# Cross attention in a decoder: scores seven pairs ahead, another order of transfers, and all key parts on POOL

## The reference

```python
Q = (query @ Wq + bq).reshape(B, Sq, H, D).transpose(0, 2, 1, 3)
K = (key @ Wk + bk).reshape(B, Sk, H, D).transpose(0, 2, 1, 3)
V = (value @ Wv + bv).reshape(B, Sk, H, D).transpose(0, 2, 1, 3)
scores = jnp.einsum('bhqd,bhkd->bhqk', Q, K) / jnp.sqrt(jnp.float32(D))
attn = jax.nn.softmax(scores, axis=-1)
out = jnp.einsum('bhqk,bhkd->bhqd', attn, V)
return out.transpose(0, 2, 1, 3).reshape(B, Sq, E) @ Wo + bo
```

## Time and profile before

| | us |
|---|---|
| median of three runs | 4712.51 (4709.47 to 4729.79) |
| the profiled execution | 4729.11 |
| its span | 4727.3 |
| PE busy | 3885.6 |
| DVE busy | 2978.1 |
| ACT busy | 2181.7 |
| POOL busy | 1144.9 |

### The profile page before, as it was taken

The page is one execution under the profiler, slowest core; times in us unless marked ns, Lnnn a source line. Parts: engine busy times, 40 slices in busy tenths (PEclk is TensorE's granted clock), DMA queues, the critical chain, the costliest instruction groups (busy, mean ns, idle before and its releaser), DMA issues. The chain is left out here.

```text
span 4727.3 us, 107462 instructions
## 1 busy us (share of the span) xinstructions
PE 3885.6 (82%) x44766; PEld 2680.4 (57%) x44766; DVE 2978.1 (63%) x4986; ACT 2181.7 (46%) x2885; POOL 1144.9 (24%) x1441
## 2 busy tenths in 40 slices
PE   7987559999996977799999979866779999995498
PEld 5864226666664446466666654333346666663376
DVE  5632468877774445488777743355668787773643
ACT  2234436656663233266666643433346666663010
POOL 0000024444440000144444410021434444430000
PEclk9989869999997999899999989978789999996689
DMA  3035035555551410355555511000045555550366
GB/s 131 0 117 201 2 88 134 139 133 137 136 135 33 115 45 0 68 140 134 139 138 138 135 44 63 24 4 4 0 108 141 134 140 137 137 129 1 81 178 159
DMA packets 251804, 463.48 MB, mean 98 GB/s; under 512 B 135598, under 2 KB 143278, under 8 KB 251086
## 3 DMA queue, kind: packets, MB, share of 16 engines
q1 hardware_dynamic: 251406, 457.76, 38.1%
HBM read 212.85 MB, written 1.72 MB: 45 GB/s over the span
## 5 line engine op out<-in xcount | busy, mean ns | idle before, releaser
L1326 DVE TENSOR_REDUCE x_bank_top<-ps 112x1 f32<-112x500 f32 x2304 | 1409.7, 670 | 457.9 <-PE ps L1055 446.2
L1184 ACT ACTIVATE x_probs_t<-ps 128x1344 f32<-128x1344 f32 x768 | 990.9, 1290 | 309.1 <-PE ps L1072 296.3
L1055 PE MATMUL ps<-x_keys,x_queries 96*112 96x500 bf16 x2304 | 697.2, 387 | 62.8 <-DVE x_bank_top L1326 34.7
L1072 PEld LDWEIGHTS ps<-x_queries,x_keys 128*128 128x128 bf16 x9216 | 504.1, 98 | 189.6 <-ACT x_probs_t L1184 90.6
L1072 PE MATMUL ps<-x_queries,x_keys 128*128 128x112 bf16 x9216 | 585.8, 213 | 30.9 <-ACT x_probs_t L1184 25.0
L1055 PEld LDWEIGHTS ps<-x_keys,x_queries 96*112 96x112 bf16 x2304 | 288.7, 131 | 391.9 <-DVE x_bank_top L1326 198.2
L1085 PE MATMUL ps<-x_probs_t,x_values 128*32 128x112 f32 x18432 | 491.2, 263 | 4.1 <-ACT x_probs_t L1184 4.1
L1085 PEld LDWEIGHTS ps<-x_probs_t,x_values 128*32 128x32 f32 x18432 | 444.4, 111 | 51.0 <-issue 43.0
L1250 POOL TENSOR_TENSOR x_key_part<-x_key_whole,x_nothing 128x500 bf16<-128x500 f32 x186 | 231.3, 1244 | 826.0 <-ACT x_key_whole L1171 826.0
L1034 PE MATMUL ps<-x_ctx_t,x_wk 128*128 128x500 f32 x558 | 311.3, 640 | 25.5 <-ACT x_key_whole L1171 15.5
L1045 PE MATMUL ps<-x_wv,x_ctx_t 128*128 128x128 f32 (+1 forms) x2304 | 328.8, 286 | 1.7 <-issue 1.6
(11 more groups left out here) (478 smaller groups left out, 5340.2 us busy)
## 6 DMA issues: line engine op xcount, KB each, us to landing
x_keys<-x_key_part SPq DMA_DIRECT2D x1152, 192.0 KB, 3.5
x_ctx_t<-in_ctx_t SPq DMA_DIRECT2D x96, 750.0 KB, 4.6
cm_ctx_n<-in_ctx_n SPq DMA_DIRECT2D x32, 768.0 KB, 6.0
cm_ctx_t<-in_ctx_t SPq DMA_DIRECT2D x32, 750.0 KB, 8.3
x_queries<-x_query_part SPq DMA_DIRECT2D x1152, 14.0 KB, 2.3
e_share<-m_weight_scratch SPq DMA_DIRECT2D x32, 490.0 KB
e_spread_out<-m_slot_scratch SPq DMA_DIRECT2D x32, 490.0 KB
e_share<-m_weight_rows SPq DMA_DIRECT2D x32, 448.0 KB, 5.8
```

Source lines behind the costliest of these rows:

```text
L1055: nc.tensor.matmul(ps[0:RW, n, 0:KB], queries[i % 2][0:TALL, p, :], keys[i % 2][0:TALL, p, KB * n:KB * n + KB], start=True, stop=True).the ...
L1072: mm = nc.tensor.matmul(ps[:, TURNED + c // VC, RW * (c % VC):RW * (c % VC) + RW], keys[i % 2][:, p, KT * c:KT * c + KT], queries[i % 2][: ...
L1184: nc.scalar.activation(probs_t[PROBS[p]].rearrange("k (n c) r -> k n (c r)", c=VC), ps[:, TURNED:TURNED + VR, 0:VC * RW], ACT.Exp, scale=s ...
L1326: nc.vector.tensor_reduce(bank_top[0:RW, p, n:n + 1], ps[0:RW, n, 0:KB], AX_X, ALU.max).then_inc(topped, 1)
```

## The change

- `LEAD` is 7 instead of 6; maxima are turned in steps 2 and 6.
- Keys are projected three batches ahead (i+3 in pass i), in steps 5 to 7 behind the scores; values of i+1 move to steps 1 to 3. Passes begin at -2.
- All three thirds are split by POOL, the maxima of half 1 between the second and the third. `last_parts` on DVE goes. POOL waits, before it writes the key parts of i, until the stack of i-2 has landed.
- Keys and queries have stacks and semaphores of their own. Queries are stacked for two batches in one transfer; in the first pass half of those transfers are issued by ACT.
- SP's order is new (below).

```diff
-LEAD = 6
+LEAD = 7
...
-    KEY_STEPS, VALUE_STEPS, FOLD_STEP = (1, 2, 3), (5, 6, 7), 4
-    BY_POOL = NB_ - 1
+    VALUE_STEPS, FOLD_STEP, KEY_STEPS = (1, 2, 3), 4, (5, 6, 7)
...
+        def query_slots(engine, e, h, s):
+
+            source = slice(64 * h, 64 * h + 64)
+            queries_of = query_parts[QUERY_PART[s]][source]
+            engine.dma_start(queries[e % 2][s:TALL:SLOTS, HP_ * h:HP_ * h + HP_].rearrange("r p b n -> r (p b n)"),
+                             queries_of[:, 2 * e:2 * e + 2].rearrange("f b c s -> f (b c s)")).then_inc(queries_stacked[e % 2][h], 16)
...
-            def stack(i, h):
+            def stack_keys(i, h):
 
                 u = i % 2
                 wait(sp, turned_done, PR * (i - 2) + HP_ * (h + 1))
                 if i == 0:
                     sp.wait_ge(lead_low, NB_)
                 else:
-                    sp.wait_ge(k_low, BY_POOL * i)
-                    sp.wait_ge(last_low, i)
+                    sp.wait_ge(k_low, NB_ * i)
...
+            def stack_queries(e, h):
+
+                wait(sp, turned_done, PR * (2 * e - 3) + HP_ * (h + 1))
+                sp.wait_ge(q_low, 2 * (2 * e // CB) + 2)
                 for s in range(SLOTS):
...
+                    query_slots(sp, e, h, s)
...
             def one_pass(i):
-                if has(i + 3):
-                    context(i + 3)
+                if i % 2 == 1 and has(i + 1):
+                    stack_queries((i + 1) // 2, 1)
                 if has(i + 2):
-                    for h in range(2):
-                        stack(i + 2, h)
-            for i in range(-1, B):
+                    stack_keys(i + 2, 0)
+                if has(i + CONTEXTS):
+                    context(i + CONTEXTS)
+                if i % 2 == 0 and has(i + 2):
+                    stack_queries(i // 2 + 1, 0)
+                if has(i + 2):
+                    stack_keys(i + 2, 1)
+            for i in range(B):
                 one_pass(i)
...
-                    wait(pe, added, min((i - 3) // CB, CH - 1))
+                    wait(pe, mix_kept, i - 3)
...
-                    if step == 3 and has(i):
+                    if step == 2 and has(i):
                         turn_tops(i, 1)
-                    if step == 7 and has(i + 1):
+                    if step == 6 and has(i + 1):
                         turn_tops(i + 1, 0)
-                    if step in KEY_STEPS and has(i + 2):
-                        make_keys(i + 2, KEY_STEPS.index(step))
+                    if step in VALUE_STEPS and has(i + 1):
+                        make_values(i + 1, VALUE_STEPS.index(step))
                     if step == FOLD_STEP and has(i - 1):
                         fold(i - 1)
-                    if step in VALUE_STEPS and has(i + 1):
-                        make_values(i + 1, VALUE_STEPS.index(step))
                     ahead, pair = divmod(step + LEAD, PR)
                     if has(i + ahead):
                         scores(i + ahead, pair)
+                    if step in KEY_STEPS and has(i + 3):
+                        make_keys(i + 3, KEY_STEPS.index(step))
...
+            act.wait_ge(q_low, 2)
+            for s in range(SLOTS):
+                query_slots(act, 0, 0, s)
...
+            def key_third(i, n):
+
+                part, cols, before = key_parts[i % 2], slice(KB * n, KB * n + KB), NB_ * (i - 1) + n
+                pool.wait_ge(k_kept, before + 1)
+                if n == 0:
+                    wait(pool, keys_stacked[i % 2][1], SLOTS * 16 * (i // 2))
...
             def one_pass(i):
...
                 if has(i + 1):
                     split_tops(i + 1, 0)
+                if has(i + 3):
+                    key_third(i + 3, 0)
+                    key_third(i + 3, 1)
+                if has(i + 1):
+                    split_tops(i + 1, 1)
+                if has(i + 3):
+                    key_third(i + 3, 2)
```

More of the change, by code:

```diff
@@ L908, in cross_attention @@
     ctx_landed = [chip.sem(tag + "ctx_landed%d" % u) for u in range(CONTEXTS)]
-    stacked = [[chip.sem(tag + "stacked%d_%d" % (u, h)) for h in range(2)] for u in range(2)]
+    keys_stacked, queries_stacked = ([[chip.sem(tag + "%s_stacked%d_%d" % (k, u, h)) for h in range(2)] for u in range(2)] for k in ("keys", "queries"))
     lead_done, lead_high, lead_rest, lead_mid, lead_low = (chip.sem(tag + k) for k in ("lead_done", "lead_high", "lead_rest", "lead_mid", "lead_low"))
@@ L944, in cross_attention @@
         key_whole = [sbuf("key_whole%d" % n, [P, KB]) for n in range(NB_)]
-        key_left = [sbuf("key_left%d" % n, [P, KB]) for n in range(2)]
+        key_left = sbuf("key_left", [P, KB])
         nothing = sbuf("nothing", [P, KB])
         keys = [sbuf("keys%d" % u, [P, PR, WIDE], BF16) for u in range(2)]
-        queries = [sbuf("queries%d" % u, [P, PR, RW], BF16) for u in range(2)]
+        queries = [sbuf("queries%d" % u, [P, PR, 2, RW], BF16) for u in range(2)]
         values = [sbuf("values%d" % u, [KT, NC_, VW]) for u in range(2)]
@@ L1005, in _ @@
                 load(dst[:], weight(name), rest_landed)
+            context(2)
             sp.wait_ge(zeros_ready, 2 * PARTS)
-            for h in range(2):
-                stack(0, h)
+            stack_keys(0, 0)
+            stack_keys(0, 1)
+            stack_queries(0, 1)
+            stack_keys(1, 0)
+            stack_keys(1, 1)
             def one_pass(i):
-                if has(i + 3):
-                    context(i + 3)
+                if i % 2 == 1 and has(i + 1):
+                    stack_queries((i + 1) // 2, 1)
                 if has(i + 2):
-                    for h in range(2):
-                        stack(i + 2, h)
-            for i in range(-1, B):
+                    stack_keys(i + 2, 0)
[6 more added lines that the diff above has]
+            for i in range(B):
                 one_pass(i)
@@ L1039, in make_values @@
                     pe.wait_ge(k_kept, NB_ * min(i + 1, B - 1))
-                    wait(pe, mix_kept, i - 1)
+                    wait(pe, mix_kept, i - 2)
+                    wait(pe, added, (i - 2) // CB)
                 else:
@@ L1049, in scores @@
                 if p % HP_ == 0:
-                    pe.wait_ge(stacked[i % 2][p // HP_], 2 * SLOTS * 16 * (i // 2 + 1))
+                    pe.wait_ge(keys_stacked[i % 2][p // HP_], SLOTS * 16 * (i // 2 + 1))
+                    if i % 2 == 0:
+                        pe.wait_ge(queries_stacked[i // 2 % 2][p // HP_], SLOTS * 16 * (i // 4 + 1))
                 if i == 0 and p == 0:
@@ L1072, in scores_by_key @@
                     mm = nc.tensor.matmul(ps[:, TURNED + c // VC, RW * (c % VC):RW * (c % VC) + RW],
-                                          keys[i % 2][:, p, KT * c:KT * c + KT], queries[i % 2][:, p, :], start=True, stop=True)
+                                          keys[i % 2][:, p, KT * c:KT * c + KT], queries[i // 2 % 2][:, p, i % 2, :], start=True, stop=True)
                 mm.then_inc(turned_done, 1)
@@ L1103, in project @@
                 pe.wait_ge(biased, c + 1)
[L1104 removed]
+                pe.wait_ge(k_kept, NB_ * min(CB * c + CB + 3, B - 1))
                 nc.tensor.matmul(ps[:, TURNS, 0:CT], wo[:], mix[:, CB * c:CB * c + CB, :].rearrange("p b s -> p (b s)"),
@@ L1144, in one_pass @@
                         mix_values(i, 0)
-            for i in range(-1, B + 1):
+            for i in range(-2, B + 1):
                 one_pass(i)
@@ L1166, in keep_keys @@
                 act.wait_ge(k_done, NB_ * (i - 1) + n + 1)
[L1167 to L1170, removed]
+                if i == 1:
+                    act.wait_ge(lead_low, n + 1)
+                wait(act, k_low, NB_ * (i - 2) + n + 1)
                 nc.scalar.activation(key_whole[n][:], ps[:, TURNS, 0:KB], ACT.Identity, bias=bk[:, 0:1]).then_inc(k_kept, 1)
@@ L1220, in one_pass @@
                         mid_query(i // 2 + 1)
-                    if step in KEY_STEPS and has(i + 2):
-                        keep_keys(i + 2, KEY_STEPS.index(step))
+                    if step in KEY_STEPS and has(i + 3):
+                        keep_keys(i + 3, KEY_STEPS.index(step))
                     if step in VALUE_STEPS and has(i + 1):
                         keep_values(i + 1, VALUE_STEPS.index(step))
-            for i in range(-1, B + 1):
+            for i in range(-2, B + 1):
                 one_pass(i)
@@ L1256, in low_parts @@
                 pool.wait_ge(k_rest, before + 1)
-                nc.gpsimd.tensor_tensor(part[1][:, cols], key_left[0][:], nothing[:], ALU.add).then_inc(k_mid, 1)
+                nc.gpsimd.tensor_tensor(part[1][:, cols], key_left[:], nothing[:], ALU.add).then_inc(k_mid, 1)
                 pool.wait_ge(k_mid, before + 1)
-                nc.gpsimd.tensor_tensor(part[2][:, cols], key_left[0][:], part[1][:, cols], ALU.subtract).then_inc(k_low, 1)
+                nc.gpsimd.tensor_tensor(part[2][:, cols], key_left[:], part[1][:, cols], ALU.subtract).then_inc(k_low, 1)
@@ L1280, in _ @@
```

(10 more changed lines are left out.)

44 lines of the change are left out of this document (7 added, 37 removed).

## The result

The changed kernel takes 5124.6 us in the median of four runs (5121.4 to 5127.2), the kernel before 4719.3 us beside it: ratio 1.0858, 95% interval 1.0829 to 1.0887. It is slower by 8.6%. Forecast were 5028 us (6.7% over the median then known) and a range of 4830 to 5160. The profiled execution took 5126.4 us, its span is 5124.7.

What follows compares the result with a forecast made beforehand. PE's own work was taken to bound the kernel before; after the change, a ring through POOL and SP's order, its links summing to 28.3 us a pass, +316 us in three stages: 5028 us, range 4830 to 5160.

Steps and rivals of the forecast that it cites:

- The ring: SP issues context i+3 behind a stack awaiting the previous batch's key parts, so each key projection waits: 28.3 us a pass.
- The links: Parts of one pass from key projection through ACT, POOL, SP's transfers and context landing to PE: sum 28.3, bounds 26.0 to 30.1.
- The first link: First key third projected on PE to ACT's start 1.15 us, ACT's start to POOL's 0.75; the low clock's 0.9 counted separately.
- link 4: Context issued to landed, right behind six key transfers: 5.2 us, bounds 4.2 and 6.6.
- the burst's lag: Transfer engines lag by 1 us, up to 2, after six key transfers; 0.6 taken into the context's landing.
- From pass to stage: 29 passes of T per stage: difference 29T - 715.5 us, +105 a stage at 28.3, +316 in three stages taken as alike.
- the stages' starts: Query transfers start some 2 us sooner, one more pair precedes first scores by key: costed at nothing, at most 3 us either way.
- PE's own way to the stack: Rival: PE's scores by key of step 3 hold the stack; low clock from about 5 us; T 30.3, 5202 us; chance 0.1.
- The light ring: Rival: transfers undisturbed and clock kept, pass 26.0 us, +38 a stage, 4828 us; chance 0.08 for under 26.5.
- the context never late: Rival: chain through POOL and SP ends before PE's step 5; PE sets the pass at 23.4, 4602 us; chance 0.06.
- the free-running pass: PE's pass with no ring: 24.4 less the 0.9 us wait for POOL's split maxima, 23.4 us.
- moving the last third from DVE to POOL: Last third of the key parts leaves DVE, which had waiting time anyway: worth nothing while PE sets the pass.

Runs made afterwards that it cites:

- experiments 1: Changed kernel with SP issuing context i+3 at the head of its pass, before any stack (the context first): 4563.9 us, ratio to before 0.9671.
- 7: Kernel before with only SP's order changed, context i+3 going out between the two halves of the stack of i+2: 5283.1 us, ratio 1.1185.
- experiment 2: Changed kernel, SP's order kept, plus one more POOL instruction of about 1.24 us in the last third of each batch's keys: 5242.6 us.
- 3: Changed kernel with the context issued before any stack, plus one more POOL instruction in each batch's last key third: 4550.9 us beside 4563.9 without it.
- experiment 8: Kernel with the context first, the last third of the keys split by DVE again in step 4: 4625.1 us beside 4556.2 without it.
- Experiment 9: Kernel with the context first, POOL splitting the second half's maxima between the first and second third of the keys: 4515.4 us, ratio to before 0.9549.
- experiment 4: Changed kernel with context i+3 issued inside the first half's key stack, behind its waits and before its six transfers: 4673.0 us, ratio 0.9912.
- experiment 5: Changed kernel with context i+3 issued between the third and fourth of the six key transfers: 5008.2 us, ratio 1.0613.

## Why the prediction was right

**The ring** was right in its place, its consequence and all its links but one: experiments 1 and 7 open and close it by SP's order alone, 2 and 3 show that length added to it counts in full only while it is closed.

**The links**, in us, in the pass shown above and on average over the 87 passes between the projections of batches 2 and 31:

| link | forecast | pass from 982.20 | mean |
|---|---|---|---|
| projection to ACT to POOL | 2.80 | 2.24 | 2.66 |
| POOL | 15.68 | 15.61 | 15.74 |
| POOL to SP | 0.09 | 0.07 | 0.08 |
| six key transfers | 4.3 | 4.24 | 4.43 |
| context's landing, PE's start | 5.4 | 6.82 | 6.13 |
| sum | 28.3 | 28.98 | 29.0 |

The first link is short in the pass shown, since the clock fell only within its projection: granted were 1.00 until 982.70 and 0.50 from 983.40. In the next pass, all at the low clock, the link took 2.83 (1011.18 to 1014.01). **The mis-sized term is link 4**, the context's landing: 5.2 us forecast, 6.1 measured. I let 0.6 of the burst's lag count. Measured, a context takes 4.6 us alone and 6.1 behind six key transfers: 1.5 us of lag, inside my bounds (up to 2.0) and not at the value I took. It accounts for most of the 0.8 us by which the pass is over my 28.3.

**From pass to stage**: 29 x 29.08 - 715.5 = +128 us for the first stage, measured +129.0. The other two grew by more, 132.7 and 137.4, because I took the stages of the kernel before as alike: its first takes 760.3 us for 31 passes, the others 753. So of the 96 us by which 5124.6 is over my 5028, about 68 are the longer pass (0.78 x 87) and 15 are the two shorter stages; the rest is in the stages' starts (1 to 3 us later each, which I had costed at nothing within 3 either way) and in the 7 us between the two medians of the kernel before. The way of the loss was forecast, and its size was not exact: 405 us where I had 316.

**PE's own way to the stack** did not decide, but was close. In the pass shown the low clock lasted 5.6 us after the gap, just past the 5 us I gave as that rival's threshold. Yet the scores by key for which the first half's stack waits ended 1.5 us before POOL's last part on average, and after it in 3 of 84 passes of the trace (batches 3 to 30 of each stage). PE's way thus took 16.9 us from the first projection, with its low clock in it, where I had put it at 16.0 without. The added POOL instruction of experiment 2 says the same: it counted with 1.19 of its 1.24 us, and had PE's way been the longer one, it would have cost less. **The light ring** and **the context never late** fall with the same rows.

**What the change gives** I underrated. I put the free-running pass at 23.4 us, from the one wait of 0.9; with the ring cut it is 22.5 to 22.6, 1.9 us under the 24.5 of before. Three things make up nearly all of it.

First, moving the last third from DVE to POOL, which I costed at nothing "while PE sets the pass", is worth 0.7 us: experiment 8 takes 69 us back, 0.74 us for each of 93 batches. But it does so in steps 5 and 6, right behind DVE's third, which holds the row maxima up; the two steps take 5.25 us together there and 4.58 with the third on POOL. In the timeline of experiment 8, start of step 5 and of step 7, with the third between:

```profile
966.70 0.41 DVE L1338 CAST x_key_part<-x_key_whole 128x500 bf16<-128x500 f32 x1
966.75 0.76 PE L1093 MATMUL ps<-x_queries,x_keys 128*128 128x112 bf16 x12
...
968.94 1.85 DVE L1349 TENSOR_REDUCE x_bank_top<-ps 112x1 f32<-112x500 f32 x3
...
972.36 0.75 PE L1093 MATMUL ps<-x_queries,x_keys 128*128 128x112 bf16 x12
```

Second, the step from 934.45 to 938.91, step 0, was 4.5 us long before and is 3.9 on average with the context first. The expectation of experiment 8 put this down to DVE's third. The traces speak against it: with the third on DVE again, step 0 still takes 3.9 us, and in the kernel before DVE had caught up by then, for it waited 0.38 us for PE just before step 0:

```profile
934.22 3.60 DVE L1326 TENSOR_REDUCE x_bank_top<-ps 112x1 f32<-112x500 f32 x6 [0.38 <-PE ps L1055]
```

So that experiment's time came out as expected for another reason, by luck. The 0.6 us of step 0 belong to another part of the change, perhaps to the scores and maxima one pair further ahead, which is the rival there; no run isolates it.

Third, the wait for POOL's split maxima fell from 0.9 us a pass to 0.4 in the kernel with the context first, and not to nothing as I had it. Experiment 9 removes the rest, and its pass is 22.0 us.

So POOL's slower instructions were right for the last third, against the page of the Trainium skill that the prediction weighed (GPSIMD Engine Reference, Performance versus the Vector engine): POOL has the room as soon as no ring goes through it.

Open: which part of the change shortens step 0.

## What to carry to other kernels

In a queue that issues in order, a transfer behind a wait inherits the wait. Before moving one, follow its data round: if what the wait stands for was made from what an earlier transfer of the same kind brought, the loop is a ring, and its sum is the least time of a pass, however idle each engine in it looks. Sum such a ring from the timeline, link by link, and compare it with the pass; here two moved lines were worth 561 of 5125 us.

## What the runs showed of the hardware that I had not expected

Here a transfer's landing depended on what was issued behind it as well as ahead. The same 750 KB took 4.6 us in the median with no key transfer close to it (the kernel before), 5.7 with six transfers of 192 KB issued right behind it (experiment 4), 6.1 right behind six (the changed kernel), and 7.4 with three on either side (experiment 5).
